# Folding the query weights of two attention branches into their keys

## The reference, cut to what matters

```
cross: q = x Wq_cr^T + bq_cr;  keys and values from x_down = conv(x, 3 taps, stride 2): 512 of them
dot:   q = x Wq_d^T + bq_d;    k = x Wk_d^T + bk_d;  1024 keys
cos:   q, k from x, each divided by its norm; 1024 keys
a = softmax(q k^T * scale);  out = layernorm(a v);  gated sum over the three branches
```

## Time and profile before

| | us |
|---|---|
| median of three runs | 1281.1 |
| span of the profiled execution, its own time (first to last instruction) | 1262.3 |
| TensorE busy / weight loads busy | 1077.9 / 954.0 |
| VectorE busy | 843.0 |
| ScalarE busy | 686.9 |
| GpSimd busy | 735.0 |
| from the start to the first scores | 65.16 |
| one block of 24 units, fourth sequence after the first two | 110.7 |
| from 940 us to the end (tail of attention, experts) | 322.3 |

### The profile page before, as it was taken

How to read it: one execution, slowest core, us unless ns; L and a number is a source line. 1 busy time by engine, 2 the same in 40 slices (tenths; PEclk the granted TensorE clock), 3 DMA queues, 4 the chain that set the end, 5 groups by cost and what they waited for, 6 DMA issues and landing times. The chain is left out here.

```text
span 1262.3 us, 23453 instructions
## 1 busy us (share of the span) xinstructions
PE 1077.9 (85%) x7553; PEld 954.0 (76%) x7553; DVE 843.0 (67%) x2699; ACT 686.9 (54%) x1765; POOL 735.0 (58%) x1188
## 2 busy tenths in 40 slices
PE   4679999999999999999999999999992367767662
PEld 3569989988989989998998999898881145556451
DVE  5356777787777867877786787777775866654210
ACT  1446756666575666667566666756653544423220
POOL 6266684766467657746765774443442045677774
PEclk9879999999999999999999999999995567799786
DMA  3010000100001101100110110000002013344442
GB/s 106 15 36 22 22 24 28 30 25 18 20 26 32 33 10 43 31 10 26 32 33 9 44 30 10 12 9 20 12 19 68 0 39 60 67 74 90 76 69 21
DMA packets 49086, 42.64 MB, mean 34 GB/s; under 512 B 6728, under 2 KB 44488, under 8 KB 48840
## 3 DMA queue, kind: packets, MB, share of 16 engines
q0 software_dynamic: 18432, 22.04, 9.3%
q1 hardware_dynamic: 30536, 19.13, 5.0%
HBM read 27.51 MB, written 13.63 MB: 33 GB/s over the span
## 5 line engine op out<-in xcount | busy, mean ns | idle before, releaser
L637 PE MATMUL mixed<-v,pT 128*128 128x131 f32 x2560 | 318.4, 276 | 0.7 <-DVE o L883 0.7
L637 PEld LDWEIGHTS mixed<-v,pT 128*128 128x128 f32 x2560 | 301.6, 191 | 0.9 <-issue 0.8
L876 DVE TENSOR_REDUCE neg_max<-scores 128x1 f32<-128x1024 f32 (+1 forms) x192 | 199.1, 1037 | 49.4 <-PE scores L439 48.8
L1107 POOL DMA_INDIRECT gram<-in_emb,ids x192 | 192.5, 1002 | 62.2 <-issue 51.8
L1035 ACT ACTIVATE probs<-scores,neg_max 128x1024 f32<-128x1024 f32 (+1 forms) x192 | 186.6, 972 | 24.9 <-DVE neg_max L876 24.6
L1044 ACT ACTIVATE pT<-turned 128x512 f32<-128x512 f32 x211 | 125.3, 594 | 64.9 <-PE turned L618 64.4
L1158 POOL TENSOR_TENSOR zb<-row,gate 128x384 f32<-128x384 f32 x64 | 54.5, 852 | 142.9 <-DVE gate L911 142.5
L437 PE MATMUL scores<-k_hi,q_hi 128*128 128x512 f32 x320 | 135.5, 423 | 2.3 <-DVE q_lo L776 2.3
L1919 POOL DMA_INDIRECT out_h<-yw,slots x64 | 102.4, 1599 | 49.1 <-DVE yw L1768 22.4
L618 PE MATMUL turned<-con,probs 128*128 128x128 f32 x844 | 123.8, 276 | 6.6 <-ACT probs L1035 1.8
L439 PE MATMUL scores<-k_hi,q_lo 128*128 128x512 f32 x320 | 126.7, 396 | 0.0
(11 more groups left out here) (306 smaller groups left out, 2445.6 us busy)
## 6 DMA issues: line engine op xcount, KB each, us to landing
wd<-in_w_down SPq DMA_DIRECT2D x32, 171.0 KB
token_table<-w SPq DMA_DIRECT2D x16, 320.0 KB, 2.4
out_h<-h SPq DMA_DIRECT2D x16, 256.0 KB, 2.3
gram<-in_emb,ids POOLq DMA_INDIRECT x192, 2.6
wu<-in_w_up SPq DMA_DIRECT2D x8, 170.5 KB, 4.2
w<-in_weights SPq DMA_DIRECT2D x1, 1174.0 KB, 7.8
xg<-token_table,slots POOLq DMA_INDIRECT x64, 2.7
out_h<-yw,slots POOLq DMA_INDIRECT x64
```

What stands on the lines that cost most here:

```text
L637: last = pe.matmul(mixed[:, 0:C + 3], pT[:, n % 2, j * P:(j + 1) * P], vals[:, 0:C + 3], start=(j == 0), stop=(last_half and j == half * 4 ...
L876: dve.tensor_reduce(neg_max[:, n % 4:n % 4 + 1], scores[:, (n % 2) * S:(n % 2) * S + width], AX_X, ALU.max, negate=True).then_inc(maxed, 1)
L1107: pool.indirect_dma_start(gram[:, t % 4, g, :], None, emb[g], bass.IndirectOffsetOnAxis(ap=ids[:, s, t, g:g + 1], axis=0)).then_inc(gather ...
```

## The change

The scores of the cross and the dot branch are (Wq x + bq)·(key). The new kernel folds Wq into the key's weights at set-up (Wk becomes Wq^T Wk, in the code a matmul of `W("k_..")` and `W("q_..")`), so that x itself is the query. For the bias of the query the kernel keeps x + 1 instead of x, and shifts the query weights so that the sum over channels gives the bias term. Whatever else reads x + 1 (convolution, k_d, qk_c, values) gets the sum of its weights subtracted from its bias (`channel_means` on TensorE, `without_means` on VectorE). The items q_d and q_cr are gone. xT has two buffers in token order; the convolution's order is a copy of its own (`xP_hi` by ScalarE, `xP_lo` by VectorE), one per half sequence.

```diff
-AHEAD_OF_LOOP = """gram0 gram1 gram2 gram3 gram4 gram5 xT0 k_d0 gram6 q_d0 q_cr0 gram7 v_dc0 gram8 qk_raw0 qk_raw1 v_dc1 v_dc2 v_dc3
-    xT1 down0 k_d1 k_cr0 qk_raw2 qk_raw3 v_cr0 v_cr1"""
+AHEAD_OF_LOOP = """gram0 gram1 gram2 gram3 gram4 gram5 xT0 k_d0 gram6 gram7 v_dc0 gram8 qk_raw0 qk_raw1 v_dc1 v_dc2 v_dc3
+    xT1 qk_raw2 qk_raw3 k_d1 down0 k_cr0 v_cr0 v_cr1"""
...
-STEADY = ("q_d1 | xT0+", "q_c1 | q_cr1", "k_d0+ | v_dc0+", "gram6+ | v_dc1+", "qk_raw0+ | v_dc2+", "gram7+ | v_dc3+",
+STEADY = ("| xT0+", "q_c1 | ", "k_d0+ | v_dc0+", "gram6+ | v_dc1+", "qk_raw0+ | v_dc2+", "gram7+ | v_dc3+",
           "qk_raw1+ |", "gram8+ |", "|", "x2T1- |", "xT1+ | route1-", "k_d1+ | qk_raw2+", "down0+ | qk_raw3+",
-          "k_cr0+ | q_d0+", "q_cr0+ | v_cr0+", "v_cr1+ | gram0++", "k_c0+ | gram1++", "k_c1+ | v_dc4+", "q_c0+ | gram2++",
+          "k_cr0+ | ", "| v_cr0+", "v_cr1+ | gram0++", "k_c0+ | gram1++", "k_c1+ | v_dc4+", "q_c0+ | gram2++",
           "gram3++ | v_dc5+", "gram4++ | v_dc6+", "x2T0 | v_dc7+", "gram5++ | route0", "|")
...
-        xT_hi = asb("xT_hi", [P, 2 * XODD], F32R)
-        xT_lo = asb("xT_lo", [P, 2 * XODD], F32R)
+        xT_hi = [asb(f"xT_hi{j}", [P, S], F32R) for j in range(2)]
+        xT_lo = [asb(f"xT_lo{j}", [P, S], F32R) for j in range(2)]
+        xP_hi = asb("xP_hi", [P, 2 * XODD], F32R)
+        xP_lo = asb("xP_lo", [P, 2 * XODD], F32R)
...
 # TensorE, at the end of setup(), ahead of gram0
+                pe.wait_ge(setup_v, 11)
+                for i, name in enumerate(("cr", "d")):
+                    pe.matmul(folded[:, i * C:(i + 1) * C], W("k_" + name), W("q_" + name), start=True, stop=True)
+                    last = pe.matmul(folded[:, 2 * C + i:2 * C + i + 1], W("q_" + name),
+                                     col[:, COL["bk_" + name]:COL["bk_" + name] + 1], start=True, stop=True)
+                last.then_inc(setup_t, 1)
+
+            def channel_means():
+                pe.wait_ge(setup_v, 16)
+                for tap in range(3):
+                    pe.matmul(col_means[:, 0:1], W("conv", tap * C, C), mean_w[:, 0:1], start=(tap == 0), stop=(tap == 2))
+                pe.matmul(col_means[:, 1:2], W("k_d"), mean_w[:, 0:1], start=True, stop=True)
+                pe.matmul(qk_means, mean_w[:], W("qk_c"), start=True, stop=True)
+                v0, v1 = WCOL["v_d"][0], WCOL["v_c"][1]
+                pe.matmul(v_means, mean_w[:], w[:, v0:v1], start=True, stop=True).then_inc(setup_t, 1)
...
             def down_item(s, dst):
-                pe.wait_ge(item_v, v_done("xT", s, 1))
+                pe.wait_ge(xP_a, s * 2 + 2)
+                pe.wait_ge(xP_v, s * 2 + 2)
...
-                lhs = q_hi[br][:, t * P:(t + 1) * P], q_lo[br][:, t * P:(t + 1) * P]
+                lhs = ((q_hi[:, t * P:(t + 1) * P], q_lo[:, t * P:(t + 1) * P]) if br == 2 else
+                       xT_tile(b, t))
...
             for k in range(PRE):
-                if ITEMS[k][0] == "k_d" and ITEMS[k][2] == 0:
+                if ITEMS[k] == ("gram", 0, 2):
+                    channel_means()
+                if ITEMS[k] == ("k_d", 0, 0):
                     pe.wait_ge(weights_ready, 1)
...
 # VectorE, setup()
-                for name in ("q_cr", "q_d"):
-                    dve.tensor_scalar(W(name), W(name), SCALE, None, ALU.mult)
-                    last = dve.tensor_scalar(col[:, COL["b" + name]:COL["b" + name] + 1],
-                                             col[:, COL["b" + name]:COL["b" + name] + 1], SCALE, None, ALU.mult)
+                for i, name in enumerate(("q_cr", "q_d")):
+                    last = dve.tensor_reduce(q_shift[:, i:i + 1], W(name), AX_X, ALU.add, negate=True)
                 step(last)
...
+                for i, name in enumerate(("q_cr", "q_d")):
+                    last = dve.tensor_scalar(W(name), W(name), float(C), q_shift[:, i:i + 1], ALU.mult, ALU.add)
+                step(last)
...
+                dve.wait_ge(setup_t, 3)
+                for i, name in enumerate(("k_cr", "k_d")):
+                    dve.tensor_scalar(W(name), folded[:, i * C:(i + 1) * C], SCALE / C, None, ALU.mult)
+                step(dve.tensor_scalar(col[:, COL["bk_cr"]:COL["bk_d"] + 1:2], folded[:, 2 * C:2 * C + 2], SCALE / C, None, ALU.mult))
+                dve.wait_ge(setup_v, 16)
...
+            def without_means():
+                dve.wait_ge(setup_t, 4)
+                for at, mean in ((col[:, COL["db"]:COL["db"] + 1], col_means[:, 0:1]),
+                                 (col[:, COL["bk_d"]:COL["bk_d"] + 1], col_means[:, 1:2]),
+                                 (R("bqk_c"), qk_means), (bias_row[:, VW:3 * VW], v_means)):
+                    last = dve.scalar_tensor_tensor(out=at, in0=mean, scalar=-float(C), in1=at, op0=ALU.mult, op1=ALU.add)
+                last.then_inc(weights_ready, 1)
...
 # VectorE, evict()
                 elif name == "xT":
-                    low(k, xT_half(xT_lo, j), by_parity(item_bank(k)), xT_half(xT_hi, j))
+                    low_bias(k, xT_lo[s % 2][:, at], item_bank(k), 1.0, xT_hi[s % 2][:, at])
+                    dve.wait_ge(item_v, V_COUNT[k + 1])
+                    if s > 0:
+                        dve.wait_ge(item_full, AT["down", s - 1, 0] + 1)
+                    dve.tensor_copy(xP_half(xP_lo, j), by_parity(xT_lo[s % 2][:, at])).then_inc(xP_v, 1)
...
-                elif name in ("q_cr", "q_d"):
...
 # ScalarE, evict()
                 elif name == "xT":
-                    high(k, xT_half(xT_hi, j), by_parity(item_bank(k)))
+                    high(k, xT_hi[s % 2][:, at], item_bank(k), 1.0)
+                    act.wait_ge(item_a, A_COUNT[k + 1])
+                    if s > 0:
+                        act.wait_ge(item_full, AT["down", s - 1, 0] + 1)
+                    act.activation(xP_half(xP_hi, j), by_parity(xT_hi[s % 2][:, at]), ACT.Identity).then_inc(xP_a, 1)
```

More of the change, by code:

```diff
@@ L52 @@
 WSPLIT = _at
-for _name, _width in (("v_nat", 3 * C), ("proj", 3 * C), ("router", NE)):
+for _name, _width in (("v_nat", 3 * C), ("q_cr", C), ("q_d", C), ("proj", 3 * C), ("router", NE)):
     WCOL[_name] = (_at, _at + _width)
@@ L242, in build_program @@
         down_lo = asb("down_lo", [P, SD], F32R)
-        q_hi = [asb(f"q_hi{i}", [P, S], F32R) for i in range(BR)]
-        q_lo = [asb(f"q_lo{i}", [P, S], F32R) for i in range(BR)]
+        q_hi = asb("q_hi", [P, S], F32R)
+        q_lo = asb("q_lo", [P, S], F32R)
         k_hi = [[asb(f"k_hi{j}_{i}", [P, S if i else SD], F32R) for i in range(BR)] for j in range(2)]
@@ L374, in build_program, with xP_half @@
         ident = con[:, 0:P]
-        def xT_half(x, half):
+        def xP_half(x, half):
             return x[:].rearrange("p (w c) -> p w c", w=2)[:, :, half * 256:(half + 1) * 256]
@@ L395, in shared_bank @@
             return (turned[:, 512:1024], mixed[:, 512:1024], turned[:, 0:512], mixed[:, 0:512])[j]
+        folded = bank(0)[:, C:4 * C]
+        col_means = bank(3)[:, C:C + 2]
+        qk_means = bank(1)[:, C:3 * C]
+        v_means = bank(2)[:, C:C + 2 * VW]
         def item_bank(k):
@@ L502, in qk_raw_item, with k_d_item @@
                     at = dst[:, j * 2 * C:(j + 1) * 2 * C]
-                    last = product(at, xT_tile(2 * i + j), split("qk_c"))
+                    last = product(at, xT_tile(s, 2 * i + j), split("qk_c"))
                 return last
             def down_item(s, dst):
-                pe.wait_ge(item_v, v_done("xT", s, 1))
-                for tap in range(3):
-                    last = product(dst, split("conv", tap * C, C),
-                                   (xT_hi[:, (XODD - 1, 0, XODD)[tap]:(XODD - 1, 0, XODD)[tap] + SD],
-                                    xT_lo[:, (XODD - 1, 0, XODD)[tap]:(XODD - 1, 0, XODD)[tap] + SD]),
-                                   tap == 0, tap == 2)
+                pe.wait_ge(xP_a, s * 2 + 2)
+                pe.wait_ge(xP_v, s * 2 + 2)
+                for tap, at in enumerate((XODD - 1, 0, XODD)):
+                    last = product(dst, split("conv", tap * C, C), (xP_hi[:, at:at + SD], xP_lo[:, at:at + SD]), tap == 0, tap == 2)
                 return last
-            def project_item(name, s, half, dst):
+            def k_d_item(s, half, dst):
                 pe.wait_ge(item_v, v_done("xT", s, half))
-                return product(dst, split(name), (xT_half(xT_hi, half), xT_half(xT_lo, half)))
+                at = slice(half * 512, half * 512 + 512)
+                return product(dst, split("k_d"), (xT_hi[s % 2][:, at], xT_lo[s % 2][:, at]))
             def k_cr_item(s, dst):
@@ L576, in item @@
                     last = down_item(s, dst)
-                elif name in ("q_d", "k_d", "q_cr"):
-                    last = project_item(name, s, j, dst)
+                elif name == "k_d":
+                    last = k_d_item(s, j, dst)
                 elif name == "k_cr":
@@ L934, in _ @@
             for k in range(PRE):
+                if ITEMS[k] == ("k_d", 0, 0):
```

(7 more changed lines are left out.)

54 lines of the change are left out of this document (24 added, 30 removed), and 6 rows, old and new, of tables (FIRST, SECOND).

## The result

The changed kernel takes 1268.65 us (median of 4, 1265.85 to 1270.73); before, in the same job, 1282.55 (4 runs). The ratio is 0.9884, with an interval of 0.9861 to 0.9906: 13.9 us less, where 15.7 were forecast.

The account below looks back on a forecast made before the run. TensorE was taken as the bound. Loop -18.5, set-up +4.4, q_d0 and q_cr0 -0.3 and order -1.3 sum to -15.7 us: span 1262.3 becomes 1246.6, plus 18.8 carried over gives 1265.4 us, range 1257 to 1275.

Parts of the forecast that it names:

- step 1: Loop on TensorE: 30 removed query items at 0.70 us each, a gain of 21.0 us.
- step 2: Slot 0: without q_d1 TensorE waits 0.70 us for the exponential in five blocks, giving back 3.5 us.
- step 3: Loop: waits for a bank held by the eviction of q_lo disappear, gain 1.5 us, bounds 0 and 3.0.
- step 4: Loop on ScalarE and VectorE: evictions go, convolution copies of 0.7 and 0.5 us come; 0.5 us lost in all.
- step 5: Set-up on TensorE: added fold and channel-means matmuls are serial with the first tokens, costing 4.4 us.
- step 7: New order ahead of the loop: first scores 1.7 us later, cosine scale 1.3 us earlier; counted as 1.3 us gained.
- step 8: Clock level in the set-up: might rise earlier or later, bounds -3 and +2 us, taken as 0.
- rival A: The clock rises in the set-up and the stalls in slot 0 don't appear: 1260 us, chance 0.18.
- Rival B: In the loop and the order ahead of it, copies and bank ring eat half the gain: 1274 us, chance 0.15.
- C: Slower: the stall in slot 0 grows until the clock falls once per block: 1300 us, chance 0.03.
- D: Loop items are worth their recorded lengths, 1.21 us per product: 1250 us, chance 0.04.
- E: TensorE isn't the bound; maxima and exponentials fill in behind removed items, only set-up is added: 1281 us, chance 0.05.

Follow-up runs that it names:

- e9: The changed kernel with nothing altered, on a chip where TensorE's signals are on time: 1251.08 us against 1264.61 for the kernel before, ratio 0.9903.
- e10: The changed kernel with q_c1 moved to slot 0 in steady blocks and the convolution's half-0 copies made behind k_d0's evictions: 1256.02 us, ratio 0.9933.
- e5: The kernel before, query items kept, with only the order of pieces ahead of the loop changed as in the changed kernel: 1261.87 us, ratio 0.9982.
- e11: The changed kernel with the old order of pieces ahead of the loop put back: 1258.10 us, ratio 0.9955 to the kernel before.
- e3: The kernel before without the 28 query items of sequences 1 to 7, nothing added: 1273.02 us, ratio 0.9906.
- e1: The kernel before, unchanged, traced again on a chip where TensorE's signals come late: 1284.92 us, ratio 0.9991.

## Why the prediction was right, and where it was not

The time was 3.3 us above the forecast and well in the range; "faster" was right. But the sum was right by errors that cancel, which is luck. The forecast's own sign says so: "The prediction is wrong if blocks save less than 1.5 us". They save 1.24 with signals on time and 0.6 with held ones. Against the trace of before, e9, also with signals on time, ends unit 191 14.2 us earlier (15.7 forecast). By parts: to the start of unit 24 it gains 4.9, where the steps add up to nothing (4.4 - 0.3 - 1.3 added, and four items of 0.7 in the first block removed); from there on it gains 9.3, where 15.7 were forecast (18.5 less those four items). The loop behind the first block was thus forecast 6.4 us too well, and the start 4.9 too badly.

1. *Items* (step 1): 0.70 each while nothing else is late: slots 13 and 14 save 1.44 for two. The sentence that failed is "The removed items of slots 1, 13 and 14 are not next to such a wait [...] they count in full." Slots 13 and 14 weren't next to one; they stood up to three slots ahead of two waits, for the cosine scale and for GpSimd's `shift`, that they had just hidden. The five steady blocks lose 1.1 to 1.2 us each by it, 5.8 of the 6.4 us.
2. *Stall in slot 0* (step 2): 0.70 forecast, 0.73 measured. Right, and with its cause.
3. *Bank waits* (step 3): the wait on `q_lo` is gone, slot 2 is 0.31 us shorter per block, some 2 us against 1.5. Right.
4. *Copies* (step 4): durations right; cost 3.2 us against 0.5, measured with held signals only, and most of it in a slot that loses nothing where signals are on time. It lies within the stated bounds of -2 to 7; the 0.5 is neither confirmed nor refuted for a chip with signals on time. The adding of 1 was taken at 0.1 us per eviction; the pass that writes xT_lo went from 0.681 to 0.692 us and the one that writes xT_hi stayed at 0.60.
5. *Set-up* (step 5): right to 0.1 us where the clock doesn't rise (e10: 4.4).
6. *q_d0 and q_cr0* (step 6) was not tried by itself.
7. *Order* (step 7): 1.3 us forecast; 2.7 (e5) and 7.0 (e11) in the medians, 4.1 and 4.65 in the profiles at unit 24. The first scores and slot 2 had the right sign, but the step stopped there: it did not ask what the shorter wait does to the 13.5 us at the lower clock behind it, though the earlier trace rows showed them.
8. *Clock* (step 8): taken as 0. It gave back 2.2 us at xn and 3.1 at the first scores; in the first trace of the changed kernel too the grams behind channel_means take 0.94 us instead of 1.65. That is the first half of rival A, which had the chance 0.18; its other half, that the stall of slot 0 doesn't appear, failed. Of eight traces with the added matmuls in their place the clock rises here in seven, and e10 shows that it can't be relied on. "TensorE: Matmul & The Clock Gate", Part 1, of the Trainium skill, which rival A cited, has activity release the clock, and adds that the number of slow matmuls at a start varies from run to run of one kernel: the seven agree with the first half. With the second agree in kind the two traces of the changed kernel with held signals, in which the clock rises at 34.1 and 33.4 us, and e9 and e10, two kernels with one set-up.

The carry-over of 18.8 us from the span to the median was no property of the kernel: 1.8 of it is what lies around the span, and 17 goes with held signals. It did no harm, since both kernels were then timed where signals are held. Rival B was right in kind (the copies come into view) and C, D and E are out: the clock stays at 1.00 in the loop, and e3 is at 0.9906. Two small slips of the working change nothing: the chances for "faster" add up to 0.86, not 0.87, and the block to 108.4, not 108.5.

## What to carry to other kernels

Before counting a removed item in full, follow the lists of the other engines for three or four slots behind it: one that is 60 per cent busy over a block can be the one that is waited for in a few slots, and a removed item there is worth only the distance to it. When a change shortens a wait in a start-up, price the stretch of lower clock that follows the wait as well as the wait. And compare the shown trace's span with the listed times first; where they are 1 per cent or more apart, use differences only, and look for waits that end in "remote" before comparing two traces line by line.

## What the runs showed of the hardware

- In two jobs of five, completion signals of TensorE come late, at places that are the same in both traces of the changed kernel: ScalarE goes on at 25.36 instead of 20.78 behind gram0 of e1, and a mix recorded until 90.49 is seen at 97.7. Before takes 1282 to 1287 us there and 1264 to 1267 elsewhere. No packets of the instruction queues fall in 18 to 26 and 90 to 98 us of e1; the cause stays open.
- The granted clock rose at 30.8 us in the set-up of e9 and not in that of e10, with equal instructions at equal distances up to there; e9's six runs spread from 1247.5 to 1256.9, e10's five from 1254.3 to 1256.5.
- In the first trace of the changed kernel the first 128-wide `u` pass of VectorE takes 0.34 to 0.35 us in 62 cases of 64, and 0.98 to 0.99 in the two in which GpSimd's `zb` starts at the same moment. In 45 of the 62 `zb` starts while `u` runs, and costs it nothing. Slot 10:

```profile
684.71 0.98 DVE L956 SCALAR_TENSOR_TENSOR u<-o,gate_r,h 128x128 f32<-128x128 f32 x1
684.71 0.83 POOL L1201 TENSOR_TENSOR zb<-row,gate 128x384 f32<-128x384 f32 x1 [4.84 <-DVE gate L948]
```
